# Inverse deviations of the expert stage: pairs of tiles on VectorE in place of GpSimd powers

## The reference

```python
x = L0_attn_x
x = _layernorm(x + attention(x), axis=-1)
x = _layernorm(x + ffn(x), axis=-1)

def _layernorm(x, axis=-1, eps=1e-05):
    m = jnp.mean(x, axis=axis, keepdims=True)
    v = jnp.var(x, axis=axis, keepdims=True)
    return (x - m) / jnp.sqrt(v + eps)

# ffn: E = 8 experts, H = 128, F = 512
expert_id = argmax(x @ wr + br)
out = gelu(x @ w1[expert_id] + b1[expert_id]) @ w2[expert_id] + b2[expert_id]
```

## Time and profile before

| | |
|---|---|
| median of 3 runs | 226.88 us (226.16 to 228.85) |
| profiled execution, its own time | 225.43 us |
| its span, first to last instruction | 223.7 us |
| TensorE, mean granted clock | 0.977 |
| busy: TensorE, VectorE, ScalarE, GpSimd | 198.0, 156.5, 146.1, 122.7 us |
| expert stage, TensorE without the attention part | about 131.6 to 214.7 us of the span |

### The profile page before, as it was taken

One profiled execution on the slowest core, in us unless ns is written; L12 is line 12 of the kernel. 1 busy time (PEld: TensorE's weight loads), 2 busy tenths in 40 slices (PEclk: granted clock), 3 DMA queues, 4 the chain that ended last, 5 costly groups with the idle time before them and its releaser, 6 DMA issues.

```text
span 223.7 us, 6040 instructions
## 1 busy us (share of the span) xinstructions
PE 198.0 (89%) x1698; PEld 155.4 (69%) x1698; DVE 156.5 (70%) x607; ACT 146.1 (65%) x379; POOL 122.7 (55%) x158
## 2 busy tenths in 40 slices
PE   7989999999999999999879969958899989789930
PEld 2768888888764555654436869948788979679930
DVE  1577677786757999999999586744746757446471
ACT  3487788888867688776845738917566666357560
POOL 8425232522795207666718655775344546666875
PEclk9999999999999999999999979999999999999985
DMA  4899999999880000111066547745575668473110
GB/s 104 241 375 413 410 414 406 407 417 403 254 250 28 0 6 24 36 36 51 26 185 200 132 143 188 199 125 151 159 213 188 167 182 221 119 198 90 30 37 7
DMA packets 28417, 40.46 MB, mean 181 GB/s; under 512 B 3497, under 2 KB 18126, under 8 KB 28384
## 3 DMA queue, kind: packets, MB, share of 16 engines
q1 hardware_dynamic: 26112, 35.80, 49.6%
q0 software_dynamic: 2272, 4.27, 5.5%
HBM read 17.95 MB, written 22.56 MB: 181 GB/s over the span
## 4 chain that ended last, share of the span: by engine, by line
PE 70%; ACT 7%; issue 6%; DVE 5%; another core or an unknown queue 4%; POOL 3%; DMA 2%; ACTq 1%; DVEq 0%; SPq 0%
PE pair L317 19%; PE pair L815 14%; PE pair L828 8%; PE bank L662 6%; ACT qfeat L991 3%; PE bank L742 3%; PE pair L765 3%; PE bank L828 3%; PE pair L742 3%; POOL out_dram L570 3%; PE pair L808 2%; PE pair L707 2%; PE bank L642 2%; PE pair L632 2%
## 5 line engine op out<-in xcount | busy, mean ns | idle before, releaser
L991 ACT ACTIVATE qfeat<-pair,w_sb 128x128 f32<-128x128 f32 x156 | 44.5, 369 | 19.7 <-PE pair L815 7.4
L815 PE MATMUL pair<-xsT,w_slot 128*128 128x128 f32 x312 | 43.1, 283 | 4.0 <-ACT xsT L981 2.0
L815 PEld LDWEIGHTS pair<-xsT,w_slot 128*128 128x128 f32 x312 | 38.6, 195 | 6.5 <-issue 4.4
L551 POOL DMA_INDIRECT sorted_rows<-x,dest x32 | 32.3, 1009 | 19.2 <-DVE dest L1219 7.6
L570 POOL DMA_INDIRECT out_dram<-x_all x26 | 26.0, 999 | 16.0 <-DVE x_all L1365 11.1
L317 PE MATMUL pair<-wkv_part,xT_all 128*128 128x256 f32 x192 | 33.7, 320 | 1.1 <-ACT vals L914 0.8
L579 POOL TENSOR_TENSOR ksum<-kfeat 128x512 f32<-128x512 f32 x12 | 16.6, 1380 | 30.4 <-DVE kfeat L1079 30.4
L828 PE MATMUL pair<-w_sb,qfeat 128*128 x232 | 31.6, 280 | 1.7 <-ACT qfeat L991 1.2
L317 PEld LDWEIGHTS pair<-wkv_part,xT_all 128*128 128x128 f32 x192 | 28.3, 188 | 4.3 <-issue 4.3
L828 PEld LDWEIGHTS pair<-w_sb,qfeat 128*128 128x128 f32 x232 | 28.8, 195 | 2.5 <-issue 2.5
L317 PE MATMUL pair<-xT_all,wq_part 128*128 128x512 f32 x72 | 24.2, 456 | 0.0
(11 more groups left out here) (202 smaller groups left out, 398.3 us busy)
## 6 DMA issues: line engine op xcount, KB each, us to landing
sorted_rows<-pad_rows SPq DMA_DIRECT2D x11, 1584.0 KB, 22.9
w_slot<-in_L_ffn_w_dram SPq DMA_DIRECT2D x39, 256.0 KB
x_all<-in_L_attn_x_dram SPq DMA_DIRECT2D x8, 256.0 KB, 4.9
w_sb<-in_L_ffn_w_dram SPq DMA_DIRECT2D x4, 512.0 KB, 13.6
x_all<-sorted_rows SPq DMA_DIRECT2D x26, 66.0 KB
xs<-sorted_rows SPq DMA_DIRECT2D x13, 66.0 KB
w_sb<-in_L_ffn_b_dram SPq DMA_DIRECT2D x1, 512.0 KB, 7.3
sorted_rows<-x,dest POOLq DMA_INDIRECT x32
```

The source lines that it names most:

```text
L551: g_.indirect_dma_start(out=sorted_rows, out_offset=bass.IndirectOffsetOnAxis(ap=dest[:, ring, i:i + 1], axis=0), in_=x1[:, ring, i, :], i ...
L815: last = mm(h_bank[t % 2][:, k * P:(k + 1) * P], w1_slot[:, t % WB, k * P:(k + 1) * P], xsT[:, t % 2, :], start=True, stop=True)
L991: a_.activation(hT[:, t % 2, k * P:(k + 1) * P], h_bank[t % 2][:, k * P:(k + 1) * P], ACT.Gelu, bias=w2_sb[:, bass.ds(w_at[t] + (FF + D + ...
```

## The change

Tiles 6 to 33 have their inverse deviation from VectorE. The first root still has four tiles (6 to 9); then come twelve pairs. A root's twelve operations lie in the two steps after its last tile, six in each: four between the step's other operations as before and two more after the moments. From step 24 on, tile s - 3 is normalised in step s (before, it was s - 6 up to step 24 and then by batches), and tiles 32 and 33 in step 35. GpSimd keeps two powers, for tiles 0 to 5 and, ahead of the store of tile 34, for tiles 34 to 36. At the end of VectorE's program tile 34 is normalised between `add_row(37)` and `add_bias(38)`, and tiles 35 and 36 after the moments of tile 37; before, tiles 35 and 36 stood there.

```diff
--- before.py
+++ after.py
@@ -356,24 +356,25 @@
         GA, GB = 4, 6
         NA, NB = [-((E * (P - 1) - g * GT * P) // P) for g in (GA, GB)]
         assert NA < XS < NB < NT and (NT - XS) * RW <= T * D and (NB - XS) * RW <= 2 * GT * D
-        BATCHES = [range(0, 6), range(22, 25), range(25, 28), range(28, 31), range(31, 33), range(33, 35), range(35, 37)]
-        ROOTS = [range(t, t + 4) for t in range(6, 22, 4)]
+        BATCHES = [range(0, 6), range(34, 37)]
+        ROOTS = [range(6, 10)] + [range(t, t + 2) for t in range(10, 34, 2)]
         ROOT_OF = {t: n for n, tiles in enumerate(ROOTS) for t in tiles}
         ROOT_STEPS = 12
-        ROOT_FROM = {tiles[-1] + 1 + i: (n, 4 * i) for n, tiles in enumerate(ROOTS) for i in range(ROOT_STEPS // 4)}
+        ROOT_FROM = {tiles[-1] + 1 + i: (n, 6 * i) for n, tiles in enumerate(ROOTS) for i in range(ROOT_STEPS // 6)}
         ALONE = BATCHES[-1][-1] + 1
         assert ALONE == NT - 2
         LAST_OF = {tiles[-1]: j for j, tiles in enumerate(BATCHES)}
         BATCH_OF = {t: j for j, tiles in enumerate(BATCHES) for t in tiles}
         LAST_ROWS = len(BATCHES[-1])
         MOST_ROWS = max(len(tiles) for tiles in BATCHES)
-        NORMALISED_IN = {s: (s - 6,) for s in range(6, 25)}
-        NORMALISED_IN |= {25: (19, 20), 26: (21, 22), 27: (23,), 28: (24,), 29: (25, 26), 30: (27,), 32: (28, 29), 33: (30,), 34: (31, 32),
-                          36: (33, 34)}
-        POWER_BEFORE = {19: 1, 24: 2, 28: 3, 29: 4, 32: 5, 34: 6}
+        NORMALISED_IN = {s: (s - 6,) for s in range(6, 18)}
+        NORMALISED_IN |= {18: (12, 13), 19: (14,), 20: (15, 16), 21: (17,), 22: (18,), 23: (19, 20)}
+        NORMALISED_IN |= {s: (s - 3,) for s in range(24, 35)}
+        NORMALISED_IN |= {35: (32, 33)}
+        POWER_BEFORE = {34: 1}
         assert MOST_ROWS <= 6
         assert sorted(t for tiles in NORMALISED_IN.values() for t in tiles) == list(range(ALONE - LAST_ROWS))
-        assert all(BATCHES[BATCH_OF[t]][-1] <= s if t in BATCH_OF else ROOTS[ROOT_OF[t]][-1] + 3 <= s
+        assert all(BATCHES[BATCH_OF[t]][-1] <= s if t in BATCH_OF else ROOTS[ROOT_OF[t]][-1] + 2 <= s
                    for s, tiles in NORMALISED_IN.items() for t in tiles)
 
 
@@ -1335,25 +1336,26 @@
                 v.tensor_scalar(ve3[:, at], mv3[:, at, 1], LN_EPS, None, ALU.add).then_inc(ve3_ready, 1)
 
             def root(n, i):
-
+                count = len(ROOTS[n])
                 at = slice(ROOTS[n][0], ROOTS[n][-1] + 1)
-                first = guess[:, 0, :]
-                now = guess[:, (i - 3) // 3 % 2, :]
-                better = guess[:, ((i - 3) // 3 + 1) % 2, :] if i < ROOT_STEPS - 1 else rstd3[:, at]
+                first = guess[:, 0, 0:count]
+                now = guess[:, (i - 3) // 3 % 2, 0:count]
+                better = guess[:, ((i - 3) // 3 + 1) % 2, 0:count] if i < ROOT_STEPS - 1 else rstd3[:, at]
+                halved, scaled_guess, less = bits_half[:, 0:count], var_guess[:, 0:count], less_half[:, 0:count]
                 reach(dve, guess_step, ROOT_STEPS * n + i)
                 if i == 0:
                     dve.wait_ge(mv3_ready, ROOTS[n][-1] + 1)
                     op = v.tensor_scalar(ve3[:, at], mv3[:, at, 1], LN_EPS, None, ALU.add)
                 elif i == 1:
-                    op = v.tensor_scalar(bits_half[:, :], ve3[:, at].bitcast(I32), 1, None, ALU.arith_shift_right)
+                    op = v.tensor_scalar(halved, ve3[:, at].bitcast(I32), 1, None, ALU.arith_shift_right)
                 elif i == 2:
-                    op = v.tensor_scalar(first.bitcast(I32), bits_half[:, :], -1.0, float(0x5F3759DF), ALU.mult, ALU.add)
+                    op = v.tensor_scalar(first.bitcast(I32), halved, -1.0, float(0x5F3759DF), ALU.mult, ALU.add)
                 elif i % 3 == 0:
-                    op = v.tensor_tensor(var_guess[:, :], ve3[:, at], now, ALU.mult)
+                    op = v.tensor_tensor(scaled_guess, ve3[:, at], now, ALU.mult)
                 elif i % 3 == 1:
-                    op = v.scalar_tensor_tensor(less_half[:, :], var_guess[:, :], -0.5, now, ALU.mult, ALU.mult)
+                    op = v.scalar_tensor_tensor(less, scaled_guess, -0.5, now, ALU.mult, ALU.mult)
                 else:
-                    op = v.scalar_tensor_tensor(better, less_half[:, :], 1.5, now, ALU.add, ALU.mult)
+                    op = v.scalar_tensor_tensor(better, less, 1.5, now, ALU.add, ALU.mult)
                 op.then_inc(guess_step, 1)
 
             def normalise_tile(t):
@@ -1389,6 +1391,8 @@
                 root_at(s, 2)
                 row_moments(s)
                 root_at(s, 3)
+                root_at(s, 4)
+                root_at(s, 5)
                 if s in LAST_OF:
                     add_row_epsilon(s)
                 normalise_tiles(s)
@@ -1627,11 +1631,12 @@
 
             last = BATCHES[-1]
             add_row(NT - 2)
+            normalise_tile(last[0])
             add_bias(NT - 1)
             row_statistics(NT - 2)
             row_moments(NT - 2)
-            normalise_tile(last[0])
             normalise_tile(last[1])
+            normalise_tile(last[2])
             add_row(NT - 1)
             row_statistics(NT - 1)
             row_moments(NT - 1)
```

## The result

Over 20 runs of each, the changed kernel has a median of 227.63 us (225.47 to 230.21), the one before 226.57 us (223.29 to 228.85). The ratio is 1.0092, 95% interval 1.0057 to 1.0127: slower by 2.1 us (1.3 to 2.9), under the 2% line. Executions of one kernel scatter by some 2%: the ratios compare the faster ones of each, so they need not equal the ratio of the medians (here 1.1 us), and a profiled one (tail_only, load_early, pairs_late) can be a slower one.

What follows compares the result with a forecast made beforehand. TensorE was taken to bound the kernel, with GpSimd's stores alone at the end. Root steps and fewer powers cost nothing, the end +0.93: 226.88 + 0.93 = 227.8 us, range 225.5 to 230.6.

Steps and rivals of the forecast that it cites:

- within 2%: Whole kernel: no difference beyond about 2% (4.5 us); chance 0.09 of slower by that, 0.04 of faster by over 2%.
- +0.93: Start of the last store: 0.30 us for tile 33's later store, 0.16 wider power, 0.47 normalisation between power and store.
- Part 1: VectorE's root steps, six root operations each: mean 1.81 us beside TensorE's 1.90, so no cost on the path.
- Rival 1: VectorE mildly the bound, added operations taking full length, from a mean step of 2.18 us: +3.2 us, 230.1; chance 0.12.
- Part 3: End of the kernel: tiles 32 and 33 normalised later, wider last power, VectorE waiting: last store at 222.0, not 221.06.
- Wrong: Signs against the forecast: additions never waiting in TensorE's undisturbed stretches, TensorE waiting, steps over 2.2, GpSimd idle before last power.
- Part 2: GpSimd loses five powers: 4.1 us of its time goes, off the path and giving nothing; the last power grows 0.16.
- 2: VectorE the bound, chained operations 0.22 us with waits not hidden, mean step 2.4: +7.0 us, 233.9; chance 0.06.
- 3: The end pulls in: step 35 short, TensorE's stop elsewhere, both stores out before the power: -0.9 us, 226.0; chance 0.10.
- 4: TensorE's stops of 1 to 3 us shift elsewhere, moving time by one stop either way; chance 0.04.

Runs made afterwards that it cites:

- tail_only: The kernel before with only the change's end (last batches, late normalisations), no pairs of roots: ratio 0.9974 to the kernel before, -0.6 us.
- load_early: The changed kernel with VectorE's register load of the weight offset moved behind the bias addition: ratio 0.9931 to the kernel before, -1.6 us.
- pairs_late: The changed kernel with both tiles of a pair normalised in the even step from step 24: ratio 0.9996 to the kernel before, -0.1 us.
- two_newton: The changed kernel with each root's third Newton step left out, 9 operations in place of 12: ratio 1.0024 to the kernel before, +0.5 us.
- load_early_2: The same kernel as load_early, measured again in another call: ratio 0.9946 to the kernel before, -1.2 us.
- early_to_31: The changed kernel with load_early's move, pairs only up to tile 31 and the end of the kernel before: ratio 0.9854 to that kernel, -3.3 us.
- wide_roots: The kernel before with VectorE's roots of four tiles carried on to tile 29, three powers fewer: ratio 0.9898 to the kernel before, -2.3 us.
- after_again: The changed kernel, unchanged, measured a second time: ratio 1.0064 to the kernel before, +1.4 us.

## Why the prediction was right, and where not

The direction, "within 2%" and the range held, and the forecast median of 227.8 is close to the 227.63 measured. That closeness is in part luck. The forecast's +0.93 came from the order at the end alone; measured were +2.1 and +1.4 us by the ratios (+1.1 and +0.7 by the medians), and the runs put the larger part down to a lateness of VectorE that the forecast had at nothing. Its parts:

- *Part 1, the length of a step.* 1.71 forecast for both halves up to step 23, and 1.79 measured where nothing disturbs them. From step 25 on 1.71 and 1.91 forecast, 2.0 and 2.1 measured. I had priced the dependent normalisation at 0.2 in all, from a row where the same thing happens; what I left out is the 0.3 us load in VectorE's queue beside it, and in the even steps the 0.2 us for which L1352 is held. Rival 1's point of decision, a mean of 2.18, came out too high: it counts all steps back to step 11, while the steps that decided are those of the last undisturbed stretch of TensorE, where anything over 1.90 adds up. "After a stop VectorE is about 1 us late and gets it back in the next" failed with it: the 1.3 us left at tile 27 stayed.
- *Part 3, "row addition of tile 35: 210.86 as before, since TensorE sets it".* This is the step that failed. It was 2.6 and 2.4 us late in two profiles, and load_early and two_newton, which take the lateness away, are about 3 us and 0.9 to 1.6 us under the changed kernel. The sign in "Wrong" that I named, additions that never wait in TensorE's undisturbed stretches, is what the trace shows.
- *Part 3, the rest.* From that addition to the last store 11.1 us forecast, 11.2 measured, so the sum along this path is right. As a cost in time the +0.93 is not borne out in full: tail_only was -0.6 us (at most +0.8), and load_early_2 against early_to_31 gives 0.3 to 0.4.
- *Part 2, five powers "off the path and gives nothing".* In doubt: wide_roots, with three powers less, was 2.3 us faster. Whether the five powers less of the change made up for part of its lateness was not tested.
- *The rivals.* 1 named the right engine with the wrong reason: operations do not lose their overlap (1.79 in the early steps). 2 and 3 didn't occur. 4, that stops of TensorE shift, is seen in every pair of profiles, also in two of one and the same kernel (changed and after_again), so none of it can be put down to an edit; what makes them isn't known.

What was shown: the lateness, by dose (9, 12, 15 operations: 0.1, 2.6, 4.3 us late) and by moving one load, and that the time goes the same way. What was only argued: the shares of the three causes of the longer step, and how much of the time the lateness makes, since two_newton and load_early differ by 2.4 us without any.

## What to carry to other kernels

An engine just under the bound in the mean is over it in the stretch that counts: compare its step with the bounding engine's undisturbed step near the end, not with a mean that has stops in it. Count a step's register loads as well as its operations; one behind a waiting instruction is exposed, and in full steps it goes best where dependent operations leave gaps (in the kernel before, whose steps had room, the same move gained nothing). Two versions measured on one chip are compared by their own times, for the difference of their ratios to a third can mislead (here 2.1 us for 0.3). And don't let an instruction need a result issued just before it, when there is other work for a step.

## What the runs showed of the hardware

The root operation L1352 (two integers per partition) has two lengths. In three traces (changed, after_again and load_early_2) it takes 0.15 us, unless it starts 0.59 us or more after the start of one of GpSimd's stores: then it is held until the store's instruction ends. Starts and lengths of the changed kernel's cases: 0.59 and 0.39, 0.63 and 0.35, 0.69 and 0.29, 0.75 and 0.23 us; all end at 0.98; at 0.52, four times, 0.14 to 0.15. Where that window begins is not fixed: in pairs_late three that started at 0.52 were held (0.46 us) and two were not. So VectorE was held until the store instruction's end, and because the store itself follows VectorE's normalisation by a fixed 0.6 us, the collision repeats in every even step once the phase is bad, as from step 26 on (in step 28 it is L1350, 0.43 us from 0.55). The Trainium skill says ("SBUF — State Buffer", Who interferes with whom) that an operation of this kind may take the port pair that VectorE shares with GpSimd, an exclusive lock. The held cases agree; those that ran through at 0.52 of the same store show that not all of the store's instruction locks.

TensorE's stops of 1 to 3 us came in every profile, in part at other places, and also in two executions of the same kernel: in the changed one step 10 took 4.1 us in one trace and 1.8 in the other. Their cause stays open.
